# One pass of statistics for two layer normalisations in a row

## The reference

```python
x = x + _L0_attn_a_ref(_layernorm(x), ...)
x = x + _L0_ffn_ref(_layernorm(x), ...)        # routed experts
x = x + _L0_attn_b_ref(_layernorm(x), ...)     # gated attention
x = x + _L0_ffn_ref(_layernorm(x), ...)        # routed experts
x = x + _L1_attn_a_ref(_layernorm(x), ...)     # state-space scan
x = x + _L1_ffn_ref(_layernorm(x), ...)
x = x + _L1_attn_b_ref(_layernorm(x), ...)
x = x + _L1_ffn_ref(_layernorm(x), ...)
```

```python
mu = mean(x); var = mean((x - mu) ** 2)
xn = (x - mu) / sqrt(var + 1e-5) * w + b       # inside the layer, on x that is normalised already
...
return result + x                              # the shortcut is the once normalised x
```

## Time and profile before

| | us |
|---|---|
| median of the runs (3104.85, 3105.89, 3114.9) | 3105.89 |
| the profiled execution | 3092.15 |
| its span, first to last instruction | 3090.4 |
| outside the span | 1.75 |
| expert stage ahead of gau, about | 1240 to 1376 |
| gau, about | 1376 to 1643 |
| expert stage ahead of mamba, about | 1643 to 1788 |
| mamba, about | 1788 to 2366 |
| mean granted clock of TensorE, share of full | 0.945 |

### The profile page before, as it was taken

How to read it: one execution, slowest core, us unless ns; L and a number is a source line. 1 busy time by engine, 2 the same in 40 slices (tenths; PEclk the granted TensorE clock), 3 DMA queues, 4 the chain that set the end, 5 groups by cost and what they waited for, 6 DMA issues and landing times.

```text
span 3090.4 us, 54695 instructions
## 1 busy us (share of the span) xinstructions
PE 2638.1 (85%) x20224; PEld 1714.0 (55%) x20224; DVE 2038.8 (66%) x4696; ACT 1696.9 (55%) x3346; POOL 912.4 (30%) x995
## 2 busy tenths in 40 slices
PE   7999899988998899678998668788766988888879
PEld 4666666665666567664446536666665622323325
DVE  5566556555665564258874248999997887777735
ACT  4776466645664566241212237877862446666662
POOL 1000020002000200443223466777875122322221
PEclk9999999999999999799999788899998989999999
DMA  5000000000000000220002111122222520110000
GB/s 181 2 2 2 1 10 2 2 1 10 2 2 1 10 2 21 62 59 18 9 9 59 48 49 62 63 70 68 71 76 85 180 97 2 56 56 2 2 2 28
DMA packets 79944, 114.24 MB, mean 37 GB/s; under 512 B 10109, under 2 KB 48172, under 8 KB 79680
## 3 DMA queue, kind: packets, MB, share of 16 engines
q1 hardware_dynamic: 71488, 97.07, 9.6%
q0 software_dynamic: 8192, 13.67, 1.6%
HBM read 77.66 MB, written 35.78 MB: 37 GB/s over the span
## 4 chain that ended last, share of the span: by engine, by line
PE 26%; issue 11%; DVE 10%; POOL 8%; another core or an unknown queue 3%; ACT 1%; DVEq 0%; POOLq 0%; SPq 0%; ACTq 0%
POOL arena L2083 6%; DVE Wqkv L2354 5%; PE ps L2230 4%; PE ps L1385 3%; PE ps L1191 3%; PE ps L688 3%; PE ps L677 2%; PE ps L2202 2%; PE ps L2191 1%; PE ps L1394 1%; PE ps L2195 1%; PE ps L1182 1%; PE ps L2239 1%; POOL arena L2066 1%
## 5 line engine op out<-in xcount | busy, mean ns | idle before, releaser
L387 ACT ACTIVATE arena<-ps 128x512 f32<-128x512 f32 (+1 forms) x640 | 333.9, 548 | 406.1 <-PE ps L291 392.3
L499 DVE CUSTOM_DVE_ANT_0 arena<-ps,causal 128x512 f32<-128x512 f32 (+3 forms) x512 | 282.2, 588 | 323.7 <-PE ps L278 286.4
L400 ACT ACTIVATE arena<-arena 128x640 f32<-128x640 f32 (+7 forms) x512 | 394.3, 771 | 37.8 <-DVE arena L499 34.1
L2354 DVE TENSOR_REDUCE Wqkv<-ps 128x2 f32<-128x1024 f32 (+3 forms) x384 | 353.1, 953 | 86.6 <-PE ps L2195 81.3
L2310 ACT ACTIVATE arena<-ps 128x1024 f32<-128x1024 f32 (+3 forms) x384 | 302.1, 809 | 162.6 <-PE ps L2202 158.9
L291 PE MATMUL ps<-ident,arena 128*128 128x128 f32 x2304 | 345.8, 283 | 46.3 <-ACT arena L400 31.9
L2083 POOL TENSOR_TENSOR arena<-arena,W 128x1024 f32<-128x1024 f32 x128 | 332.6, 2618 | 133.8 <-DVE W L2035 133.8
L1791 PE MATMUL ps<-rope,arena 128*128 128x128 f32 x2048 | 282.2, 300 | 96.2 <-ACT rope L1930 48.1
L291 PEld LDWEIGHTS ps<-ident,arena 128*128 128x128 f32 x2304 | 254.3, 142 | 161.7 <-issue 87.5
L312 PE MATMUL ps<-arena,rope 128*64 128x128 f32 x4608 | 341.5, 284 | 0.0
L1791 PEld LDWEIGHTS ps<-rope,arena 128*128 128x128 f32 x2048 | 267.9, 213 | 126.3 <-issue 72.0
(11 more groups left out here) (265 smaller groups left out, 4272.3 us busy)
## 6 DMA issues: line engine op xcount, KB each, us to landing
select<-c_rows SPq DMA_DIRECT2D x64, 512.0 KB, 3.6
arena<-q_dram SPq DMA_DIRECT2D x4, 2048.0 KB, 9.0
arena<-k_dram SPq DMA_DIRECT2D x4, 2048.0 KB, 14.2
q_dram<-arena SPq DMA_DIRECT2D x24, 256.0 KB, 3.7
k_dram<-arena SPq DMA_DIRECT2D x24, 256.0 KB, 3.8
arena<-slots_in SPq DMA_DIRECT2D x8, 640.0 KB, 6.6
slots_out<-arena SPq DMA_DIRECT2D x8, 640.0 KB, 4.3
slots_in<-select SPq DMA_DIRECT2D x4, 640.0 KB, 6.3
```

Source lines behind the costliest of these rows:

```text
L387: nc.scalar.activation(k.probT[:, n % 2, b0 * P:(b0 + nb) * P], k.ps[:, 4 + m % 2, 0:nb * P], ACT.Copy)\
L400: nc.scalar.activation(k.prob[:, i % 2, h, 0:w], k.prob[:, i % 2, h, 0:w], ACT.Exp, bias=k.neg_max[:, i % 2, h:h + 1], scale=-1.0, accum_o ...
L499: ins = nc.vector.tensor_tensor_reduce(k.prob[:, i % 2, h, 512 * g:512 * g + w], k.ps[:, banks[h], 0:w], k.causal[:, first:first + w], 1.0 ...
L2354: nc.vector.tensor_reduce(k.least[:, g, a, i % 4, c, :], k.ps[:, 2 * (m % 3):2 * (m % 3) + 2, 0:search_width(i, c)], AX_X, ALU.min)\
```

## The change

`dve_norm_piece` has 8 pieces in place of 13. Statistics are taken of X alone. From variance v, `twice_var` = v (1 + eps) + eps^2 and `var_eps` = v + eps are both made in piece 2, and their powers -1/2 are `twice_rstd` (power `ln` 0) and `rstd` (power `ln` 1). Pieces 3 and 4 write twice normalised rows straight from X. Piece 5 makes two small columns, `kept_gain` = rstd + 1 and `kept_shift` = mean * rstd. Pieces 6 and 7 replace X by X * gain - shift, four tiles each. The step o_b of gau is piece 8. The small columns lie in the tile `XN`, which these layers no longer fill.

```diff
-NORM_BESIDE = ((0, 1), (2,), (4,), (5, 6), (7, 8), (10,), (11,), (12, 13))
+NORM_BESIDE = ((0, 1), (2,), (3,), (4,), (5,), (6,), (7,), (8,))
...
     def next_roots(c, t):
-        if (c, t) in ((0, 7), (1, 5)):
+        if (c, t) in ((0, 7), (1, 0)):
             pool_norm_root(nc, k, pool, next_sm, 0, c)
...
-    if piece in (0, 1, 6, 7):
-        for t in range(4 * (piece % 2), 4 * (piece % 2) + 4):
-            last = nc.vector.bn_stats(k.bn6[:, t, :], (k.X_all[:, 8 * b + t, :] if piece < 2 else k.XN[:, t, :]))
+    if piece in (0, 1):
+        for t in range(4 * piece, 4 * piece + 4):
+            last = nc.vector.bn_stats(k.bn6[:, t, :], k.X_all[:, 8 * b + t, :])
         ch.link(last)
-    elif piece in (2, 8):
+    elif piece == 2:
         for t in range(8):
             last = nc.vector.bn_aggr(k.mv[:, t, :], k.bn6[:, t, :])
         ch.link(last)
-        nc.vector.tensor_scalar(k.var_eps[:], k.mv[:, :, 1], EPS, None, ALU.add).then_inc(sm[("var1", "var2")[piece // 8]], 1)
-    elif piece in (4, 5, 10, 11):
-        dve.wait_ge(sm[("rstd1", "rstd2")[piece // 10]], b + 1)
-        if piece == 10 and b >= 1:
+        nc.vector.tensor_scalar(k.twice_var[:], k.mv[:, :, 1], 1.0 + EPS, EPS * EPS, ALU.mult, ALU.add)\
+            .then_inc(sm["var2"], 1)
+        nc.vector.tensor_scalar(k.var_eps[:], k.mv[:, :, 1], EPS, None, ALU.add).then_inc(sm["var1"], 1)
+    elif piece in (3, 4):
+        dve.wait_ge(sm["rstd2"], b + 1)
+        if piece == 3 and b >= 1:
             dve.wait_ge(sm["xnT_ps"], 2 * b)
...
+        for t in range(4 * (piece - 3), 4 * (piece - 3) + 4):
+            last = nc.vector.tensor_scalar(out[:, t, :], k.X_all[:, 8 * b + t, :], k.mv[:, t, 0:1], k.twice_rstd[:, t:t + 1],
+                                           ALU.subtract, ALU.mult)
+        last.then_inc(sm["xn2"], 1)
+    elif piece == 5:
+        dve.wait_ge(sm["rstd1"], b + 1)
+        ch.mark(nc.vector.tensor_scalar(k.kept_gain[:], k.rstd[:], 1.0, None, ALU.add))
+        ch.link(nc.vector.tensor_tensor(k.kept_shift[:], k.mv[:, :, 0], k.rstd[:], ALU.mult))
+    elif piece in (6, 7):
+        for t in range(4 * (piece - 6), 4 * (piece - 6) + 4):
+            X = k.X_all[:, 8 * b + t, :]
+            last = nc.vector.tensor_scalar(X, X, k.kept_gain[:, t:t + 1], k.kept_shift[:, t:t + 1], ALU.mult, ALU.subtract)
+        ch.link(last)
...
+G_NORM_PIECES = {0: 0, 1: 1, 2: 2, 5: 3, 6: 4, 7: 5, 8: 6, 9: 7, 10: 8}
...
+S_NORM_PIECES = {1: 0, 2: 1, 4: 2, 7: 3, 8: 4, 9: 5, 10: 6, 11: 7}
...
-        if n in (3, 9) and b + 2 < k.B:
-            pool_norm_root(nc, k, pool, sm, b + 2, n // 9)
+        if n in (5, 6) and b + 2 < k.B:
+            pool_norm_root(nc, k, pool, sm, b + 2, n - 5)
```

More of the change, by code:

```diff
@@ L1086, in pe_tokens @@
+def pool_norm_root(nc, k, pool, sm, b, ln):
+    if ln == 0:
+        pool.wait_ge(sm["var2"], b + 1)
+        nc.gpsimd.tensor_tensor(k.twice_rstd[:], k.twice_var[:], k.minus_half[:], ALU.pow).then_inc(sm["rstd2"], 1)
+    else:
+        pool.wait_ge(sm["var1"], b + 1)
+        nc.gpsimd.tensor_tensor(k.rstd[:], k.var_eps[:], k.minus_half[:], ALU.pow).then_inc(sm["rstd1"], 1)
 def pe_tokens(nc, k, pe, sm, b, src):
@@ L1268, in dve_gau_norm @@
     dve_norm_piece(nc, k, dve, ch, sm, b, piece, k.XN2)
-    if piece == 13:
+    if piece == 8:
         X = k.X_all[:, 8 * b:8 * b + 8, :]
@@ L1316, in dve_gau @@
             if b + 1 < k.B:
-                dve_gau_norm(nc, k, dve, ch, sm, b + 1, u)
+                dve_gau_norm(nc, k, dve, ch, sm, b + 1, G_NORM_PIECES.get(u))
             elif u in (4, 5, 6):
@@ L2008, in norm_piece @@
         dve_norm_piece(nc, k, dve, ch, sm, b, piece, k.XN2s)
-    for piece in range(13):
+    for piece in range(8):
         norm_piece(1, piece)
@@ L2462, in build @@
         k.rstd = sb("rstd", [P, 8])
+        k.twice_var, k.twice_rstd, k.kept_gain, k.kept_shift = (k.XN[:, 0, 8 * n:8 * n + 8] for n in range(4))
         first_loads, loads, late_loads = [], [], []
@@ L2837, in mamba_norm @@
             def mamba_norm(b, piece):
-                if piece < 13:
+                if piece < 8:
                     dve_norm_piece(nc, k, dve, ch, k.S, b, piece, k.XN2s)
```

16 lines of the change are left out of this document (2 added, 14 removed).

## The result

The change was forecast at -8.1 us and made the kernel slower. In the first comparison it took 3115.91 us (median of 11 runs, 3109.01 to 3125.22) against 3105.89 (11 runs), a ratio of 1.0036 with a 95% interval of 1.002 to 1.0052. Three repeats gave 1.0049 (1.0031 to 1.0067), 1.0058 (1.0029 to 1.0086) and 1.0056 (1.0027 to 1.0086). By these ratios the loss is 11 to 18 us; the 0.3% that was taken as the limit of a measurement is 9.3. Ratios are those of mean times, so they are not exactly the quotients of the medians given, and the one of the last repeat leaves out two runs of the changed kernel (3131.55 and 3135.64) that lie over 1.5% above its fastest.

The account below looks back on a forecast made before the run. VectorE was taken to bound mamba's scans, PE gau and the expert stages. Terms -11.4 - 2.0 + 3.9 + 1.4 = -8.1 took the median 3105.89 to 3097.8, range 3090 to 3108.

Parts of the forecast that it names:

- Expert stages, a gain of 2.0: Both expert stages: VectorE's wait for the second power and PE's idle time of 2.03 go; only the second stage's gain is kept.
- The second stage's is, -2.0: the way into mamba goes over PE and ACT: Second expert stage, ahead of mamba: its gain of 2.0 us is kept, since PE and ACT set the way into mamba.
- rival D: Mamba's start: PE arrives 2.0 earlier, its first groups run into the denser gathers; slower, 3108; chance 0.08.
- Gau, batch 0, +3.9: Gau's first batch: piece 5 waits at u = 7 for rstd behind the gathers; PE 2.9 late plus 1.0 for its clock.
- The clock's +1.0: Gau's first batch: after standing, PE's granted clock drops and its matmuls lose 1.0 us.
- Gau, batches 1 and 2, +1.4: Gau's batches 1 and 2: more VectorE work ahead of `hot` (L842) lengthens PE's wait at L655, +0.7 each.
- The scans, -11.4: Mamba's scans, bound by VectorE: batches with pieces become 124.0, gaining 6.4 in batch 0 and 5.0 in batch 1.
- Whatever VectorE does at n = 7 to 10 is swallowed: Mamba's scans, steps 7 to 10: pieces cost nothing, as a PE and ACT chain sets the stretch; 1.7 of waiting left.
- The collision with GpSimd at n = 12: Mamba's scans: VectorE loses 3.2 to GpSimd with or without a piece there; removing the piece brings some 1.4.
- B: Gau's first batch: its wait never reaches PE, so the sum is -14, 3092; chance 0.16.
- C: Mamba's scans: pieces 3 and 4 at n = 7 and 8 collide with GpSimd's sums, +8, giving 3106; chance 0.12.
- E: Mamba: another engine takes over at once, batches 0 and 1 stay near 128, sum about 0, 3105; chance 0.10.

Follow-up runs that it names:

- experiment 3: One pass of statistics in the expert stages alone or gau alone, against the kernel before: 1.0015 each without late increments (quiet chip), 1.0132 and 1.0025 with them.
- experiment 4: Most early expert-stage gathers became fills with zero: kernel before 2982.17, changed kernel 2977.01 (chip without late increments); changed kernel 0.9877 of the kernel before (chip with them).
- experts_only: Kernel before with one pass of statistics only in the last batch of either expert stage: 3001.38 (1.0015); again on a chip with late increments 3122.27 (1.0132).
- after_fills: Changed kernel with gathers of the second to fourth batch of both early expert stages made fills: 2977.01, against 2982.17 for the kernel before with the same fills.
- experiment 6: One pass in mamba's loop alone, pieces 5 and 6 both at n = 9, piece 7 at n = 10 instead of 11: 3094.66, 0.9975 of the kernel before.
- scan_only: Kernel before with one pass of statistics only in mamba's loop (batches 2 and 3): 3095.96 (0.9969), again 3096.02 (0.9986).
- scan_packed: Mamba's loop alone with one pass, its last piece at n = 10 instead of n = 11: 3094.66, 0.9975 of the kernel before.

## Why the prediction was wrong

**The sign fell on the expert stages.** "Expert stages, a gain of 2.0" is the step that failed. The two waits did vanish, and on the quiet chip the last batches were 3.3 shorter each. But "The second stage's is, -2.0: the way into mamba goes over PE and ACT" was wrong even there: it goes over the root behind GpSimd's gathers, and what PE gained it stood longer in mamba's head (experiment 3). And what the prediction put at nothing is what PE's timing does beside GpSimd's gathers: with increments up to 13 us late, a last batch became 4 to 6 longer and gau's first batch 10. The kernel before shows the same thing in mamba's head, and the prediction used these rows for rival D alone and only for that place; there the changed kernel lost nothing. D had the right mechanism at the wrong place. That GpSimd's DMAs bring the lateness is shown (experiment 4), and that the large loss comes with the expert stages' part is shown by the times of experiment 3. That lateness makes the whole of this loss is argued from the waits in the traces. Why the new arrangement falls into the long stretches in some executions isn't settled: the moved root is part of it at most.

**Gau, batch 0, +3.9** was right in its mechanism (all of gau's part is +4.2 on the quiet chip, where 3.9 + 1.4 was forecast): rstd late by 7.25 and 7.26, PE idle 2.1 to 2.8 and 0.5. The clock's +1.0 doesn't show: the halves behind these waits took 1.98 each. What was missed is that the first root stands behind gathers too: with the earlier PE of the changed expert stages VectorE waits 7.07 for it (experts_only), and PE stands 4.78.

**Gau, batches 1 and 2, +1.4**: on the quiet chip 68.8 against 67.9 or 68.0, +0.8 each, with PE's wait at L655 1.99 and 2.00 where 1.95 was forecast. On the others batch 1 was +2.5 or more, and on the quiet chip it took 72.1 in after_fills, +4.2, with the same 1.99 at L655; so late increments aren't needed for that, and its cause is open.

**The scans, -11.4**, measured -7.7. Steps 1 to 6 are as worked out (-2.5 and -2.3). "Whatever VectorE does at n = 7 to 10 is swallowed" is the step that failed: the stretch from n = 7 to 11 took 33.9 in batch 0 and 34.5 in batch 1, where 32.4 was taken, and up to 35.2 and 36.1 in the other traces. In batch 1 it isn't even shorter than before (33.7 to 34.5). PE's L1801 behind step 7 was fast, 4.14 as in batch 2, so that assumption held. The reading of the timelines is that pieces at n = 7 and 8 push back the next scans, PE's matmuls wait for these, and ACT's chain waits for what stands behind them on PE; no run took the two pieces away alone. Both timelines of the changed kernel:

```profile
1974.86 4.14 PE L1801 MATMUL ps<-rope,arena 128*128 128x128 f32 x32 [1.61 <-DVE W L2034]
1978.93 1.98 PE L1764 MATMUL ps<-Wqkv,WdtT 16*128 16x512 f32 x4
```

```profile
1980.95 1.11 ACT L1903 ACTIVATE W<-ps,s_cols 128x1024 f32<-128x1024 f32 x1 [1.13 <-PE ps L1764]
```

In batch 2 of the kernel before the same ACT instruction waited for nothing:

```profile
2197.07 1.10 ACT L1893 ACTIVATE W<-ps,s_cols 128x1024 f32<-128x1024 f32 x1
```

A piece at n = 10 is indeed free in batch 0 (experiment 6). The collision with GpSimd at n = 12 was seen rightly as one that stays (products 4.15 in batch 0, 6.02 in batch 1, where 5.6 was forecast); that in batch 0 a freed slot at n = 11 or 13 hands the collision to the products, was not.

The prediction also misread how large that collision is. It set 3.6 us against one GpSimd instruction of 1.99, and took this as more than the blocking rule allows. There were two, L2066 and right behind it L2069; each held up one of the four operations of piece 11 by about its own length (2.09 and 2.15 in place of 0.33). VectorE's and GpSimd's timelines of the kernel before:

```profile
1966.44 2.09 DVE L1070 TENSOR_SCALAR Wo<-XN,mv,rstd 128x128 f32<-128x128 f32 x1
```

```profile
1968.52 2.00 POOL L2069 TENSOR_TENSOR W<-arena,W 128x1024 f32<-128x1024 f32 x1
```

Rivals: B did not come; C did not (pieces 3 and 4 took 1.56 and 1.09 in batch 0); E did not. The chances gave slower 0.07; all four comparisons are slower by more than 0.3%.

The version that beats both kernels is the loop of mamba alone: scan_only 0.9969 and 0.9986, scan_packed 0.9975, by 0.14 to 0.31% (the interval of 0.9986 reaches 1.0005).

## What to carry to other kernels

An edit that removes waits ahead of a stretch with GpSimd's DMAs is not worth what the waits were: price what the engine meets when it comes earlier, a root tied to a gather's place and increments that are seen late. Where the trace has waits whose releaser it can't name, list them by stage before forecasting, and treat each stage that has them as uncertain by their size. Change one stage at a time; here the part with the clear gain was worth 8 us alone and was buried under the rest.
